# Layer 2 cross attention: the third batch's keys and values before the second's scores, the output projection among the last batches; layer norm rows by two engines

## The reference, cut to what matters

```python
def _layernorm(x, axis=-1, eps=1e-05):
    m = jnp.mean(x, axis=axis, keepdims=True)
    v = jnp.var(x, axis=axis, keepdims=True)
    return (x - m) / jnp.sqrt(v + eps)

def _L2_xattn_ref(Q, K, V, Wq, bq, Wk, bk, Wv, bv, Wo, bo):   # 16 heads of 16
    q = (Q @ Wq + bq) / T
    k = K @ Wk + bk
    v = V @ Wv + bv
    scores = jnp.einsum('bqhd,bkhd->bhqk', q, k)
    attn = jax.nn.softmax(scores, axis=-1)
    out = jnp.einsum('bhqk,bkhd->bqhd', attn, v).reshape(b, -1, D_MODEL)
    return out @ Wo + bo

x = x + _L2_xattn_ref(_layernorm(x), ctx_1024, ctx_1024, ...)
```

## Time and profile before

| | |
|---|---|
| median of 3 runs | 1978.56 us (1977.77 to 1979.53) |
| the profiled execution's own time | 1979.34 us |
| its span | 1977.6 us, mean granted clock 0.963 |
| busy | PE 1811.5 us (92%), DVE 1075.2 (54%), ACT 808.4 (41%), POOL 564.9 (29%) |
| layer 2's cross attention | 1154.7 to 1373.7 us on the span's clock |

### The profile page before, as it was taken

The page is one execution under the profiler, slowest core; times in us unless marked ns, Lnnn a source line. Parts: engine busy times, 40 slices in busy tenths (PEclk is TensorE's granted clock), DMA queues, the critical chain, the costliest instruction groups (busy, mean ns, idle before and its releaser), DMA issues. The chain is left out here.

```text
span 1977.6 us, 43225 instructions
## 1 busy us (share of the span) xinstructions
PE 1811.5 (92%) x16810; PEld 1405.4 (71%) x16810; DVE 1075.2 (54%) x2695; ACT 808.4 (41%) x2340; POOL 564.9 (29%) x617
## 2 busy tenths in 40 slices
PE   8999779999999889799999989998588899987898
PEld 6886569844777756699999957776454477755787
DVE  7787841352366337875555545555665555437511
ACT  6663621122266334233333325553410566616232
POOL 4441313100144202311121113331311466515242
PEclk9999889999999999999999999998699999998899
DMA  4120068560233110041899641111011355300397
GB/s 146 55 56 5 3 239 296 192 217 30 57 102 100 28 54 3 8 195 58 310 330 334 225 169 50 50 45 54 2 54 57 89 157 155 102 1 2 109 338 253
DMA packets 87010, 233.92 MB, mean 118 GB/s; under 512 B 9776, under 2 KB 45136, under 8 KB 80304
## 3 DMA queue, kind: packets, MB, share of 16 engines
q1 hardware_dynamic: 78992, 213.90, 32.1%
q0 software_dynamic: 5664, 15.47, 2.5%
q10 hardware_dynamic: 2176, 2.10, 0.3%
HBM read 216.21 MB, written 12.07 MB: 115 GB/s over the span
## 5 line engine op out<-in xcount | busy, mean ns | idle before, releaser
L2190 POOL TENSOR_TENSOR l1x_probs<-l1x_probs,l1x_total 128x512 f32<-128x512 f32 x64 | 65.0, 1038 | 211.4 <-DVE l1x_total L2415 211.4
L1515 PE MATMUL PS<-weights,l0x_ctxT 128*128 128x256 f32 x512 | 121.0, 386 | 0.8 <-DVE l0x_kp L1803 0.7
L1048 PE MATMUL PS<-l1f_xT,l1f_slot 128*128 128x128 f32 x1024 | 117.0, 275 | 0.0
L1048 PEld LDWEIGHTS PS<-l1f_xT,l1f_slot 128*128 128x128 f32 x1024 | 115.7, 192 | 0.1
L1515 PEld LDWEIGHTS PS<-weights,l0x_ctxT 128*128 128x128 f32 x512 | 94.0, 190 | 15.9 <-issue 3.5
L2923 POOL TENSOR_TENSOR l2x_probs<-l2x_probs,l2x_total 128x512 f32<-128x512 f32 x64 | 65.1, 1038 | 136.3 <-DVE l2x_total L3097 136.3
L81 PE MATMUL PS<-consts 128*128 128x256 f32 x340 | 85.1, 403 | 17.5 <-PEq L87 15.8
L81 PEld LDWEIGHTS PS<-consts 128*128 128x128 f32 x340 | 67.5, 203 | 31.6 <-issue 19.5
L235 ACT ACTIVATE std<-moments,eps 128x8 f32<-128x8 f32 x13 | 3.9, 301 | 203.1 <-DVEq L173 133.7
L1175 DVE SCALAR_TENSOR_TENSOR l1f_product<-PS,l1f_slot,l1f_side 128x128 f32<-128x128 f32 x128 | 36.0, 344 | 65.9 <-ACT l1f_side L1131 50.9
L3401 PE MATMUL PS<-l3x_keysT,l3x_QW 128*128 128x289 f32 x256 | 67.7, 407 | 1.7 <-issue 1.7
(11 more groups left out here) (659 smaller groups left out, 4648.5 us busy)
## 6 DMA issues: line engine op xcount, KB each, us to landing
l1f_slot<-in_experts_up_dram SPq DMA_DIRECT2D x16, 2056.0 KB
weights<-in_experts_up_dram SPq DMA_DIRECT2D x8, 2056.0 KB, 7.8
weights<-in_experts_down_dram SPq DMA_DIRECT2D x21, 640.0 KB, 4.3
weights<-in_experts_up_dram SPq DMA_DIRECT2D x10, 1024.0 KB
l1f_slot<-in_experts_down_dram SPq DMA_DIRECT2D x16, 640.0 KB, 4.1
l0x_ctxT<-in_ctxT_dram SPq DMA_DIRECT2D x32, 257.0 KB, 2.6
l1x_ctxT<-in_ctxT_dram SPq DMA_DIRECT2D x32, 257.0 KB
l2x_ctxT<-in_ctxT_dram SPq DMA_DIRECT2D x32, 257.0 KB, 2.6
```

The source lines that it names most:

```text
L1048: done = nc.tensor.matmul(PS[:, bank + a, m * P:(m + 1) * P], mat[:, c, m * P:(m + 1) * P], x, start=(c == 0), stop=(c == 1))
L1515: last = nc.tensor.matmul(PS[:, 2 * (b % 2) + k, half * D:(half + 1) * D], ctxT[b % SLOTS][:, c, half * P:(half + 1) * P], kw[:, c, k * D: ...
L2190: nc.gpsimd.tensor_tensor(p, p, bcast(total[b % 2][:, 2 * n:2 * n + 2], 2, KEYS), ALU.mult).then_inc(probs_done, 1)
```

## The change

1. **Rows by two engines.** In the eleven uses of the head in layer 0's self attention, and in all of layers 1, 2 and 3 (layer 3's self attention has two), VectorE first computes shift = -mean x rstd (128x8), then writes tiles 0, 2, 4, 6 and 7; ScalarE waits for the shift and writes tiles 1, 3 and 5 as Identity(rstd x + shift), ahead of everything else in its list there. rows_done becomes a pair of semaphores, and all who waited for it wait for both.
2. **Layer 0's feed forward.** The sum of X and H moves behind find_rows.
3. **Layer 2's cross attention.** keys_values(2), with ScalarE's and VectorE's copies, comes before sim(1); flip_probs(0) waits for these copies. GpSimd adds bo to all of X at the start. The output projection uses banks 0 to 3: tiles 0 and 1 before the last flip_probs, tile 2 before the last weigh, 3 to 5 after it, 6 and 7 when AT is complete. VectorE adds tiles 0 and 1 before the last keep_own.

The diff, cut (the rest changes rows_done to a pair and adds norm.scalar_rows behind norm.scalar in each of these parts):

```diff
+ROWS_BY_DVE, ROWS_BY_ACT = (0, 2, 4, 6, 7), (1, 3, 5)
...
     def rows(self, dve, src, dst, rows_done):
...
+        dve_done, _ = rows_done
+        self.shifts_dve += 1
+        nc.vector.scalar_tensor_tensor(c.shift[:], c.moments[:, :, 0], -1.0, c.rstd[:], ALU.mult, ALU.mult).then_inc(self.shift_done, 1)
+        for t in ROWS_BY_DVE:
             nc.vector.tensor_scalar(dst[:, t, :], src[:, t, :], c.moments[:, t, 0:1], c.rstd[:, t:t + 1],
-                                    ALU.subtract, ALU.mult).then_inc(rows_done, 1)
+                                    ALU.subtract, ALU.mult).then_inc(dve_done, 1)
+
+    def scalar_rows(self, act, src, dst, rows_done):
+        c, nc = self.core, self.core.nc
+        _, act_done = rows_done
+        self.shifts_act += 1
+        act.wait_ge(self.shift_done, self.shifts_act)
+        for t in ROWS_BY_ACT:
+            nc.scalar.activation(dst[:, t, :], src[:, t, :], ACT.Identity, bias=c.shift[:, t:t + 1], scale=c.rstd[:, t:t + 1]).then_inc(act_done, 1)
+
+    def wait_rows(self, eng, rows_done):
+        dve_done, act_done = rows_done
+        eng.wait_ge(dve_done, len(ROWS_BY_DVE))
+        eng.wait_ge(act_done, len(ROWS_BY_ACT))
...
@@ l0_feed_forward, vector
-            dve_step(dve, nc.vector.tensor_tensor(core.X[:], core.X[:], core.H[:], ALU.add))
             flip.vector(dve, XT)
...
             ex.places.find_rows(dve)
+            dve_step(dve, nc.vector.tensor_tensor(core.X[:], core.X[:], core.H[:], ALU.add))
             ex.vector(dve)
...
@@ l2_cross, gpsimd
+            pool.wait_ge(core.x_in, 16)
+            norm.wait_rows(pool, rows_done)
+            nc.gpsimd.tensor_tensor(core.X[:], core.X[:], bcast(bo, 1, NT), ALU.add).then_inc(x_shifted, 1)
...
@@ l2_cross, tensor
-                    if o == 0 and b >= 2:
+                    if o == 0 and b >= 3:
                         pe.wait_ge(pt_copied_act, b - 1)
...
-                if b >= 2:
+                if b >= 3:
                     pe.wait_ge(pt_copied_dve, b - 1)
...
                 pe.wait_ge(probs_done, 2 * b + 2)
+                if b == 0:
+                    pe.wait_ge(k_copied, 6)
+                    pe.wait_ge(v_copied, 3)
...
+            def project(tiles):
+                for t in tiles:
+                    for c in range(C):
+                        done = nc.tensor.matmul(PS[:, t // 2, (t % 2) * D:(t % 2 + 1) * D], AT[:, c, t * P:(t + 1) * P],
+                                                wo[:, c, :], start=(c == 0), stop=(c == 1))
+                    if t % 2:
+                        done.then_inc(out_done, 1)
+
             sim(0)
+            keys_values(2)
             for b in range(B):
                 if b + 1 < B:
                     sim(b + 1)
+                else:
+                    pe.wait_ge(exps_done, 2 * B)
+                    project((0, 1))
                 flip_probs(b)
-                if b + 2 < B:
+                if b + 2 < B and b:
                     keys_values(b + 2)
+                if b == B - 1:
+                    project((2,))
                 weigh(b)
+            project((3, 4, 5))
             pe.wait_ge(at_done, B)
...
+            project((6, 7))
+            core.keep_busy(4, 4)
...
@@ l2_cross, scalar
             exps(0)
+            copy_keys(2)
             for b in range(B):
                 copy_probs(b)
...
@@ l2_cross, vector
+            def add_out(n):
+                x = core.X[:, 2 * n:2 * n + 2, :]
+                dve.wait_ge(x_shifted, 1)
+                dve.wait_ge(out_done, n + 1)
+                written = nc.vector.tensor_tensor(x, PS[:, n, :].rearrange("p (t d) -> p t d", t=2), x, ALU.add)
+                norm.take(dve, written, (2 * n, 2 * n + 1))
+
             tops(0)
             weights(0)
+            copy_values(2)
...
+            add_out(0)
             keep_own(B - 1)
-            dve.wait_ge(at_done, B)
-            for n in range(NT // 2):
-                x = core.X[:, 2 * n:2 * n + 2, :]
-                dve_step(dve, nc.vector.tensor_tensor(x, x, bcast(bo, 1, 2), ALU.add))
-                dve.wait_ge(out_done, n + 1)
-                written = nc.vector.tensor_tensor(x, PS[:, 4 + n, :].rearrange("p (t d) -> p t d", t=2), x, ALU.add)
-                norm.take(dve, written, (2 * n, 2 * n + 1))
+            for n in range(1, NT // 2):
+                add_out(n)
```

More of the change, by code:

```diff
@@ L56, in __init__ @@
         self.rstd = self.sb("rstd", [P, NT])
+        self.shift = self.sb("shift", [P, NT])
         self.warm = self.sb("warm", [P, 1])
@@ L165, in __init__ @@
         self.std_done = core.sem("norm_std_done")
-        self.uses_dve = self.uses_act = 0
+        self.shift_done = core.sem("norm_shift_done")
+        self.uses_dve = self.uses_act = self.shifts_dve = self.shifts_act = 0
         self.taken = False
@@ L247, in __init__, with tensor @@
         self.uses = {"pe": 0, "act": 0, "dve": 0}
-    def tensor(self, pe, src, rows_done, before, order=None):
+    def tensor(self, pe, src, rows_done, order=None):
         c, nc = self.core, self.core.nc
@@ L258, in tensor @@
                 for t in range(4 * half, 4 * half + 4):
-                    pe.wait_ge(rows_done, before + t + 1)
+                    if isinstance(rows_done, tuple):
+                        if t in ROWS_BY_ACT:
+                            pe.wait_ge(rows_done[1], ROWS_BY_ACT.index(t) + 1)
+                        else:
+                            pe.wait_ge(rows_done[0], ROWS_BY_DVE.index(t) + 1)
+                    else:
+                        pe.wait_ge(rows_done, t + 1)
                     to, rows = c.PS[:, 2 * half + ch, (t % 4) * P:(t % 4 + 1) * P], src[:, t, ch * P:(ch + 1) * P]
@@ L961, in load @@
             tiles = slice(4 * half, 4 * half + 4)
-            sp.wait_ge(rows_done, 4 * half + 4)
+            if isinstance(rows_done, tuple):
+                sp.wait_ge(rows_done[0], sum(t < 4 * half + 4 for t in ROWS_BY_DVE))
+                sp.wait_ge(rows_done[1], sum(t < 4 * half + 4 for t in ROWS_BY_ACT))
+            else:
+                sp.wait_ge(rows_done, 4 * half + 4)
             sp.dma_start(self.rows_dram.rearrange("(t p) d -> p t d", p=P)[:, tiles, :], rows[:, tiles, 0:D]).then_inc(self.rows_stored, 16)
@@ L1990, in _ @@
             norm.scalar(act, core.eps5)
+            norm.scalar_rows(act, core.X, core.H, rows_done)
             flip.scalar(act, core.HT)
@@ L2324, in _ @@
             norm.scalar_twice(act)
+            norm.scalar_rows(act, core.X, core.H, normed_done)
             flip.scalar(act, core.HT, ln_g, ln_b)
@@ L3007, in _ @@
                     sim(b + 1)
+                else:
+                    pe.wait_ge(exps_done, 2 * B)
+                    project((0, 1))
                 flip_probs(b)
-                if b + 2 < B:
+                if b + 2 < B and b:
                     keys_values(b + 2)
+                if b == B - 1:
+                    project((2,))
                 weigh(b)
+            project((3, 4, 5))
             pe.wait_ge(at_done, B)
-            for t in range(NT):
-                for c in range(C):
-                    done = nc.tensor.matmul(PS[:, 4 + t // 2, (t % 2) * D:(t % 2 + 1) * D], AT[:, c, t * P:(t + 1) * P],
-                                            wo[:, c, :], start=(c == 0), stop=(c == 1))
-                if t % 2:
-                    done.then_inc(out_done, 1)
-            core.keep_busy(0, 4)
+            project((6, 7))
+            core.keep_busy(4, 4)
         @block.scalar
@@ L3276, in _ @@
             flip.vector(dve, core.HT)
-            dve.wait_ge(rows_done, NT)
+            norm.wait_rows(dve, rows_done)
             nc.vector.tensor_tensor(core.X[:], core.X[:], core.H[:], ALU.add)
```

71 lines of the change are left out of this document (44 added, 27 removed).

## The result

The changed kernel takes 1970.20 us (median of 9 runs, 1963.05 to 1975.58) where the kernel before, run beside it, takes 1978.56 (9 runs, 1973.59 to 1982.61). The ratio is 0.9952, 95% interval [0.9938, 0.9966]: faster by 9.5 us, interval 6.7 to 12.3. The forecast was 1974.0 and the range 1967 to 1980, so the direction and the range held, while the gain is twice the 4.6 us that were summed. The profiled execution took 1972.36 us (span 1970.6, mean granted clock 0.965).

A forecast was written before the change was run, and what follows sets the result against it. TensorE computes nine tenths of the span, but stages have different limits (rows, transposes, waits). Terms -1.9-3.3-6.8+7.4 = -4.6 us against the profiled 1979.34 give 1974.7, put at 1974.0 for the median; range 1967 to 1980.

The forecast's parts named there:

- A: Layer norm rows by two engines in eleven heads: -1.9 us, bounds -4.5 and +1.
- C: End of layer 2's cross attention, bias on GpSimd and projection in earlier waits: -6.8 us, bounds -3.5 and -7.2.
- D: Start of layer 2's cross attention, batch 2's keys wait for their context: +7.4 us, bounds +4.5 and +10.
- B: Layer 0's feed forward, moved sum of X and H lets the router start earlier: -3.3 us, bounds -1.9 and -3.4.
- five rivals: Transfer in time 0.08, clock decides 0.20, GpSimd held up 0.08, two-engine rows bring nothing 0.07, slower by the loop 0.05.
- rival 2: Clock decides in layer 2's cross attention, half clock after the pause or in the tail: 1976.5 to 1977.3; chance 0.20.
- The order's 4.3: Layer 2's cross attention start: keys before batch 1's scores and batch 0's transposes lose 4.3 us.
- The transfer's +1.1: Layer 2's cross attention start: last_raw copied after ScalarE's three rows delays the V_last loads by 1.1 us.
- The clock's term: Layer 2's cross attention start: batch 2's keys and values mostly at half clock, 2.0 us, bounds 0 and 4.5.
- Rival 1: Layer 2's cross attention start: batch 2's context is there in time, the start costs 0; 1966.6; chance 0.08.
- The clock's 1.4: Layer 0's feed forward: the router, starting earlier, is through before the clock falls, -1.4 us.
- Rival 3: Layer 0's feed forward: moved sum holds up GpSimd's gathers, up to 2.28 us return; 1976.3; chance 0.08.

The follow-up runs named there:

- run 8: Kernel before plus only the layer norm rows by two engines: 1976.97 us, ratio 0.9979 to the kernel before.
- run 6: Kernel before plus only GpSimd's bias and the output projection among the last batches of layer 2's cross attention: 1970.69 us, ratio 0.9948 to the kernel before.
- run 5: Kernel before plus only batch 2's keys and values ahead of batch 1's scores: 1987.48 us, ratio 1.0033 to the kernel before.
- run 10: Changed kernel with layer 0's sum of X and H back at its old place: 1972.43 us, ratio 0.9960 to the kernel before.
- run 2: Changed kernel with SyncE issuing batch 2's context behind the third of four V_last loads: 1963.75 us, ratio 0.9921 to the kernel before.
- run 7: Changed kernel with the old end of layer 2's cross attention (projection, bias and adds as before): 1982.77 us, ratio 1.0013 to the kernel before.
- run 4: Changed kernel with batch 2's keys and values at their old place, its context transferred early, last_raw copied before ScalarE's rows: 1967.67 us, ratio 0.9944 to kernel before.
- run 1: Changed kernel with batch 2's keys and values back at their old place: 1966.67 us, ratio 0.9927 to the kernel before.
- run 11: Changed kernel with layer 0's sum of X and H in VectorE's wait for the router: 1971.03 us, ratio 0.9955 to the kernel before.

## Why the prediction was right, and where its sizes were off

The sum of the parts by time is -4.2 (A, run 8) -10.3 (C, run 6) +6.5 (D, run 5) = -8.0 us, against -9.5 for the whole, which leaves -1.5 to B. B was not run alone; taking it out (run 10) gives -1.6, so by time the four parts add up within the intervals, each some 2 to 2.5 us wide to either side. At the start of layer 2's cross attention A and D are not independent, as the traces show below. None of the five rivals took the place of the forecast; the clock, rival 2's subject, moved terms in both directions. To land in the range was no close hit: the gain is twice the forecast, and that it is not further off is owed to B's miss, which goes against the others.

**Part D, +7.4 forecast.** Every step that it names is in the changed kernel's trace: keys wait for the context (8.44 us idle, forecast "from about 1174.5 to 1183"), SyncE's chain starts later, the clock falls, the loop's period stays 5.69 (1195.20 for the third transposes behind 1189.51). In the changed kernel's trace the 9.5 us that the second transposes come later are 2.2 of transfer (keys at 29.36 us from the root, before 27.19), 3.0 of clock and 4.3 of order. The order's 4.3 was exact. The other two terms are not the order's alone: run 8 has the old order and shows 2.2 of transfer and 2.9 of clock as well, from ScalarE's rows ahead of the copy of last_raw, or from chance in the loads and the clock. Added to rows by two engines, the new order costs just 41.54-37.23 = 4.3 us; added to the kernel before (run 5) it costs 6.6 with 2.3 of clock and no later transfer. The prediction asked for the clock only behind its long pause and not what rows by two engines do there by themselves. The transfer's +1.1 held for the copy (2.27 us after the root, before 1.16), but the four loads took 16.23 instead of 14.91 us. With rows by two engines they took 14.0 to 16.3 in five other traces, without 14.8 to 15.0 in three, so that part of the delay isn't settled. The clock's term, 2.0 in the text, was 3.0 in this trace, 2.3 in run 5 and 1.4 (run 7) to 3.0 in all six traces with the new order and the late transfer. With the old order it was 0 in the two traces with rows by one engine and 1.2 to 2.9 in the three with rows by two (runs 4, 1 and 8); why the clock falls there is open. By time D alone is 6.5 [4.2, 8.9]. The Trainium skill ("TensorE: Matmul & The Clock Gate", on oscillation in real kernels) was right in kind: behind the waits of 8.44 us (changed kernel) and 6.41 us (run 5) for the transfer the keys' passes ran at a granted clock of 0.50, the values' at 0.6 and 0.8. Rival 1 (the transfer in time) is what run 2 makes of the kernel, and its forecast of 1966.6 is 3 us above the 1963.75 that it took.

**Part C, -6.8 forecast.** The part itself gained 7.1, within 0.4 of the sum. The mis-sized term is what follows it: I gave the next self attention 0.8 (in A) and the feed forward behind it nothing. Run 6, which has no rows by two engines, shows 1.1 and 0.9. In its trace both heads run at full clock, where those of the earlier trace rows were below it: the prediction read 0.5 in both, and the windows of the same trace have 0.59 for the self attention's (1376.50 to 1379.30) and 0.50 for the feed forward's. Only the self attention's gain goes with the end in every trace. By time the end is worth 10.3 [7.7, 12.7].

**Part A, -1.9 forecast, 4.2 [2.2, 6.1] gained by time.** Two steps failed. ScalarE's row takes 0.592 us by its group (forecast 0.55) with a pitch of (1.59-0.59)/2 = 0.50 (0.46), and VectorE's five rows take 1.70: these were right. But the full-clock heads gained 0.52 to 0.37 us, most of them more than 0.36, since the shift delays the first row by 0.09 us (184.37 to 184.46) where the sum had 0.24, and the transposes follow the last row closely and this comes 184.46+1.70 = 186.16, that is 2.02 us behind the reciprocal's start (before 2.92). And the half-clock heads do not lose 0.24: layer 3's two gain 0.2 to 0.3, and layer 2's feed forward no longer runs at half clock. In layer 3's self attention the changed kernel's trace gives some back: its first four passes behind the second norm take 3.56 us (granted clock 0.54) where they took 1.96, and from there to the feed forward it needs 72.05 us instead of 69.36. In ten traces with rows this stretch takes 68.1 to 72.5, in four without 69.4 to 71.0, so it isn't settled that the rows do it. Layer 2's cross attention is the larger loss: 5.2 us in run 8's trace and 3.1 in run 1's, of which the prediction knew 1.1 and put it into D. The head sums (3.8) less such losses fall short of what the times say; where the rest is gained stays open. Nor do layer 1's 3.7 us in the first table settle it: its three parts together take 757.0 to 762.6 us in the ten traces with rows by two engines and 759.8 to 763.2 in the four without.

**Part B, -3.3 forecast.** At the router it was right: from the root to the first distances 13.04 us (265.31), before 16.6. Of these 3.5 us, 2.7 are left at the second expert. The clock's 1.4 in it rests on one trace of each kernel, though: two of the nine traces with the sum moved had the router at a lower clock all the same. Rival 3 (0.08) happened in kind, the gather's issue 1.94 us longer, but not in size: with the clash taken away (run 11) the second expert starts 0.6 us earlier, and from the root 3.3 us earlier than before, the forecast to the tenth. The reason was not the one that the prediction set against the rival (late weights), but the clock of the first expert's passes. The Trainium skill's rule on the shared interfaces ("GPSIMD Engine Reference", Key points) was right in kind. The rest is the unsettled difference between a trace and the times: by time B is -1.5 by difference and -1.6 (interval 4 us to either side) by run 10.

The sum missed 4.9 us: 2.3 in A, 3.5 in C, 0.9 in D, against 1.8 the other way in B. In C, the clock of the head behind a filled wait should have been counted as a gain of its own, as it was counted as a loss in D. The 1.1 us of the transfer, counted in D, belonged to A, and A had no term for the clock behind it.

## What to carry to other kernels

Before moving work ahead in an engine's order, look where its transfer stands in the queue that issues it: here the same reordering cost 6.5 us by itself (run 5), and with one moved transfer the cost was gone (run 2). Look also at what is put ahead of a copy that starts a chain of transfers: rows by two engines delayed last_raw by 1.1 us, and in the two traces with the old order and the late transfer the second transposes came 3 and 5 us later. Where short waits are filled at an end of a part, look also at the head of the next part, which here gained 1.1 us by the clock. And where the clock moves some us between executions of one kernel, read a part's length from several traces before giving a difference to an edit. An instruction of VectorE with two SBUF operands should lie where GpSimd has nothing to do, though what it holds up matters only if nothing else is later.

## What the runs showed of the hardware

VectorE and GpSimd held each other up, in both directions, until the other's instruction was nearly or fully over. GpSimd's 1.20 us issue of a gather took 3.14 beside VectorE's sum of two SBUF tensors and ended at 282.16, 1.07 us behind the sum's end at 281.09. The other way round, VectorE's 32x256 sum of two SBUF tensors takes 0.40 us alone; beside GpSimd's 128x2048 sum, timeline of run 6:

```profile
1157.24 4.52 POOL L2956 TENSOR_TENSOR X<-X,weights 128x2048 f32<-128x2048 f32 x1 [2.92 <-DVE tagged L195]
...
1159.39 2.64 DVE L3120 TENSOR_TENSOR l2x_last_rows<-l2x_last_raw,weights 32x256 f32<-32x256 f32 x1
```

It ends at 1162.03, 0.27 us behind GpSimd's 1161.76; in the changed kernel it ended at 1155.31, 0.28 behind GpSimd's 1155.03. VectorE's copies from PSUM beside the same sum kept their 0.69 us. The Trainium skill ("SBUF — State Buffer", Who interferes with whom) describes the shared ports as an exclusive lock; these rows agree.
